# Trainium2, one core: a chunk loop with its state products ahead of the next turn and no special first tiles, SP transfers in another order, attention heads in row tiles of 64

## Chip, cores and metric

The kernel runs on one core of one Trainium2 chip, in one launch. The time is device microseconds (us) for the whole program, the median of a few runs. Engine names are those of the profile: PE is TensorE's matmuls, PEld its weight loads, DVE VectorE, ACT ScalarE, POOL GpSimd, SP SyncE, which here only issues DMA transfers.

## What is computed

Two transformer layers on `x` of 4 sequences of 1024 tokens, width 128, in f32. The first layer's mixer is a gated delta rule with a fast and a slow state per head (16 heads, keys and values of 64), beside a feed-forward layer in emulated FP4. The second layer is causal attention (16 heads of 8) beside a top-1 mixture of 8 experts. Cut to what matters:

```python
def step(carry, x):                       # once a token, S_f = S_s = 0 at a sequence's start
    S_f, S_s = fd * S_f, sd * S_s
    err_f = vt - einsum('bhk,bhkv->bhv', kt, S_f)      # err_s alike
    S_f, S_s = S_f + beta * kt[:, None] * err_f, S_s + beta * kt[:, None] * err_s
    S_fc, S_sc = _cap(S_f + rf * S_s), _cap(S_s + rf * S_f)
    return (S_fc, S_sc), fg * (qt @ S_fc) + sg * (qt @ S_sc)
...
x = x + mixer(layernorm(x)) + fp4_ffn(layernorm(x))
attn = where(triu(k=1), -inf, einsum('bnhd,blhd->bhnl', q, k))
x = x + softmax(SCALE * attn) @ v @ Wp.T + bp + top1_moe(layernorm(x))
```

## The kernel before

The program goes through its stages one after the other. All engines run their own instruction streams, written out in program order and tied by semaphores. By the time in the profiled span: layer norm and FP4 feed-forward (0 to 360 us), projections (360 to 652), key products, gate recurrences on DVE and the transfers that lay their results out (652 to 845), the chunk loop (845 to 2690), output projection, layer norm, routing and experts (2690 to 3061), attention (3061 to 3694) and a last projection.

**The chunk loop.** The 4096 tokens are T = 32 tiles of 128 (TB = 8 to a sequence), and a tile is 4 groups of four heads, so k runs over GROUPS = 128 groups; `first(k)` is true for the groups of tiles 0, 8, 16 and 24, where a sequence starts with a zero state. Inside a tile the delta rule is solved as a triangular system. Its inverse is built up by levels: `lower(k, lv)` (L955) and `update(k, lv)` (L966) on PE for lv 0, 1, 2, with ACT copying each `lower` out (`xs`, L1121) and DVE folding each `update` in (`keep_update`, L1307 for levels 0 and 1, L1305 `tw` for level 2). `solve(k)` (L988) multiplies by that inverse. `turn(k + 1)` (L918) transposes the next group's queries and keys, `states(k, w)` (L978) multiplies the old state `S_t` by keys (w = 0) and queries (w = 1), `scores` (L927) makes the products of keys and queries, `change` (L999) the change of the state, `answers` (L1007) and `values0` (L1016) the output, and `factors` (L936, L939) the decay factors, from `cft`, `lt` and `rt_src`. On DVE `new_state(k - 1, step)` (L1350, L1352, L1354, L1356) forms the new state in steps 0 to 2 and `put_output` (L1374, L1378, L1379) the output; on POOL L853 squares the state and L825 and L826 scale the inverse's parts. `turn(0)` waits for the end of the stage before on each engine (`end_phase`, L479).

The order on PE is `scores(k)`, `change(k-1)`, `lower(k,0)`, `answers(k-1)`, `update(k,0)`, `values0(k-1)`, `lower(k,1)`, `turn(k+1)`, `update(k,1)`, `states(k,0)`, `lower(k,2)`, `states(k,1)`, `update(k,2)`, `factors(k+1)`, `solve(k)`. For a first group `states` and `answers` are left out, `change` is 128 columns narrower, and DVE copies instead of adding.

**SP's queue in the loop.** For tile i SP waits for the tile before last (`av_mm`, `s_new`) and then issues `load_tile(i)` (qkv, `rt_src`, `lt`, `xc`, `blk`, `cft`). Every fourth tile (i = 4, 8, ..., here called a part tile; PT = 4) it also stores the small inverses that DVE worked out during the last four tiles, `store_part(c)` (L650), and loads the next part's blocks, `load_part(c + 1)` (L645), 32 transfers. `INVERSE` spreads the rows of the inverse over the 16 groups of a part.

**Attention.** 32 steps (8 pairs of head sets for 4 sequences), each with 8 query tiles t and 8 key tiles. `for_maxima` (L1849, mask L1851) makes the scores of two heads (e = 0, 1) for a query tile, DVE takes row maxima (L2396), PE turns them (L1859), DVE subtracts them from the queries (`q_less`, L2403), `for_weights` (L1869, mask L1871) makes scores with keys on the rows, ACT takes exponentials (L2087), and `values` (L1887) multiplies by the values. The units share three PSUM slots. Both heads of a pair lie in one 128-row operand, q of head e in rows 64e to 64e + 63; `k_pad` holds k twice, once for each e, with zeros in the other head's 64 rows, so that each matmul contracts over 128 rows:

```python
last = pe.matmul(at[:, e, 0:w], q_parts[:, n, m, t * P:t * P + P], k_pad[:, n, e, m, 512 * c:512 * c + w], ...)
if c == t // 4:
    last = pe.matmul(at[:, e, w - P:w], ident_b[:, :], above[:, :], start=False, stop=True)
```

## Time and profile before

| | |
|---|---|
| median of 3 runs | 3739.81 us |
| lowest and highest | 3722.52 and 3745.09 us |
| the profiled execution's own time | 3714.81 us |
| its span (first to last instruction) | 3713.2 us |
| PE busy | 3009.4 us, 81% of the span |
| DVE, ACT, POOL busy | 70%, 43%, 33% |
| chunk loop, stage 845 to 2690 us | 1845 us |
| attention, stage 3061 to 3694 us | 633 us |

The profile shows one execution. An engine's busy share is an average over stages of different limits; what ends a stretch is read from the row of the instruction that waits. A timeline's row merges consecutive instructions of one line: start, duration, engine, line, operation, operands (for a matmul the tile of weights as rows*columns, here rows of the PE array times columns), count, and in brackets the idle time just before with what ended it. PEclk is the granted clock of TensorE as a share of 2.4 GHz: 1.00 is that level, 0.50 the lower one of 1.2 GHz.

### The profile page before, as it was taken

How to read it: one execution, taken by the hardware profiler on the slowest of the kernel's cores; microseconds unless marked ns; L12 is line 12 of the kernel's file. 1: busy time of each engine (PE TensorE's matmuls, PEld its weight loads, DVE VectorE, ACT ScalarE, POOL GpSimd, SP SyncE). 2: the span in 40 equal slices, each digit the busy share in tenths (PEclk: the TensorE clock that was granted, in tenths of full speed). 3: DMA queues.
4: the chain of work that ended last, by engine and by line, in shares of the span. 5: the costliest groups of instructions: out<-in, count | busy, mean ns of one | idle time of the engine just before them, and what ended most of it. 6: DMA issues, size and time to landing. Idle time of an engine off the chain costs nothing. (4 is left out here: it accounts for less than half of the span.)

```text
span 3713.2 us, 74163 instructions
## 1 busy us (share of the span) xinstructions
PE 3009.4 (81%) x27767; PEld 2108.0 (57%) x27767; DVE 2588.0 (70%) x4506; ACT 1590.6 (43%) x3559; POOL 1226.3 (33%) x1881
## 2 busy tenths in 40 slices
PE   0566999657989979899798997999946388999888
PEld 0444443546767767677676776777735283333334
DVE  8895888873757747587475874766668647777775
ACT  0233999662333323233232332333334254555554
POOL 0000233113545535455354553555546503000000
PEclk9776999885989969899798997999979799999999
DMA  1001665790231312222222222222156322111011
GB/s 28 0 1 61 233 237 243 231 242 30 54 72 35 72 35 60 53 54 62 45 59 54 53 60 47 60 68 46 47 192 211 129 81 45 22 18 27 18 18 32
DMA packets 491495, 290.77 MB, mean 78 GB/s; under 512 B 404955, under 2 KB 451611, under 8 KB 482589
## 3 DMA queue, kind: packets, MB, share of 16 engines
q1 hardware_dynamic: 481920, 256.61, 25.4%
q10 hardware_dynamic: 4608, 16.78, 1.5%
q0 software_dynamic: 4608, 12.59, 1.0%
q8 instruction: 225, 3.69, 0.4%
q14 instruction: 134, 1.10, 0.1%
HBM read 155.92 MB, written 129.97 MB: 77 GB/s over the span
## 5 line engine op out<-in xcount | busy, mean ns | idle before, releaser
L2396 DVE TENSOR_REDUCE mx<-banks 128x2 f32<-128x1024 f32 (+3 forms) x384 | 360.7, 956 | 150.0 <-PE banks L1849 110.7
L2087 ACT ACTIVATE probs<-banks 128x1024 f32<-128x1024 f32 (+3 forms) x384 | 310.2, 811 | 286.6 <-PE banks L1871 156.2
L1121 ACT COPY xs<-banks 64x64 f32<-64x64 f32 (+2 forms) x640 | 166.5, 260 | 597.2 <-PE banks L955 594.2
L1307 DVE SCALAR_TENSOR_TENSOR xc<-xc,halves,banks 64x64 f32<-64x64 f32 (+1 forms) x512 | 160.2, 313 | 271.0 <-PE banks L966 265.2
L955 PE MATMUL banks<-xc,ssm 64*64 64x16 f32 (+2 forms) x5120 | 264.6, 223 | 49.7 <-issue 42.8
L988 PE MATMUL banks<-stk,tw 128*128 128x192 f32 x1024 | 269.5, 422 | 39.2 <-DVE tw L1305 39.2
L955 PEld LDWEIGHTS banks<-xc,ssm 64*64 64x64 f32 x5120 | 222.5, 141 | 127.3 <-issue 63.6
L1729 PE MATMUL banks<-wproj,xnT 128*128 128x512 f32 x512 | 265.4, 600 | 0.9 <-DVE sb_tok L2172 0.9
L1149 ACT COPY ah<-banks 128x768 f32<-128x768 f32 x128 | 102.3, 799 | 381.7 <-PE banks L988 381.7
L826 POOL TENSOR_SCALAR xc<-xc,halves 128x64 f32<-128x64 f32 (+1 forms) x256 | 135.4, 529 | 391.0 <-DVE xc L1307 378.4
L988 PEld LDWEIGHTS banks<-stk,tw 128*128 128x128 f32 x1024 | 220.0, 243 | 64.1 <-DVE tw L1305 59.1
L1111 ACT COPY ssm<-banks 16x64 f32<-16x64 f32 (+2 forms) x896 | 216.7, 242 | 75.6 <-PE banks L927 63.4
L1869 PE MATMUL banks<-q_less,k_pad 128*128 128x512 bf16 (+3 forms) x768 | 204.0, 329 | 51.5 <-DVE mx L2396 50.9
L833 POOL TENSOR_TENSOR ag<-ah,gt_sb 128x512 f32<-128x512 f32 x128 | 174.4, 1363 | 200.1 <-ACT ah L1149 200.1
L1600 POOL TENSOR_TENSOR prj_sq<-prj 128x1024 f32<-128x1024 f32 x32 | 77.5, 2422 | 491.4 <-ACT prj L1990 491.4
L1849 PE MATMUL banks<-k_pad,q_parts 128*128 128x512 bf16 (+3 forms) x768 | 205.5, 331 | 6.3 <-DVE mx L2396 3.3
L966 PE MATMUL banks<-xs,ttw 64*64 64x32 f32 (+1 forms) x3072 | 188.4, 236 | 12.6 <-ACT xs L1121 7.9
L966 PEld LDWEIGHTS banks<-xs,ttw 64*64 64x64 f32 x3072 | 155.1, 148 | 62.4 <-ACT xs L1121 45.4
L1887 PE MATMUL banks<-probs,vaug 128*9 128x256 f32 (+3 forms) x1920 | 184.2, 424 | 0.0
L918 PE MATMUL banks<-ident,qkv_t 128*128 128x128 f32 x512 | 94.0, 312 | 106.8 <-DMA cft<-cf_s 72.5
L927 PE MATMUL banks<-kqt 64*128 64x256 f32 x1024 | 172.6, 463 | 0.0
L1350 DVE TENSOR_TENSOR zs<-S_t,banks 128x256 f32<-128x256 f32 x112 | 47.1, 421 | 179.6 <-PE banks L999 178.7
(351 smaller groups left out, 7012.4 us busy)
## 6 DMA issues: line engine op xcount, KB each, us to landing
proj_s<-prj SPq DMA_DIRECT2D x32, 2048.0 KB, 6.7
qkv_t<-proj_s SPq DMA_DIRECT2D x32, 1536.0 KB
ka<-proj_s ACTq DMA_DIRECT2D x32, 512.0 KB, 4.7
mem_s<-o_sb SPq DMA_DIRECT2D x32, 512.0 KB, 2.6
om<-mem_s SPq DMA_DIRECT2D x32, 512.0 KB, 3.9
om<-proj_s SPq DMA_DIRECT2D x32, 512.0 KB, 4.9
nblk_s<-ssa POOLq DMA_DIRECT2D x32, 256.0 KB, 3.9
blk_s<-res SPq DMA_DIRECT2D x16, 512.0 KB, 4.1
```

The source lines that it names most:

```text
L833: pool.tensor_tensor(ag[:, :, :], ah[:, k % 2, :, 0:P], gt_sb[:, k % 2, :, :], ALU.mult).then_inc(ag_set, 1)
L927: last = pe.matmul(bk[m % 2][:, 256 * p:256 * p + 256], kqt[r, k % 2, p, 0, :], kqt[r, k % 2, p, :, :].rearrange("p w t -> p (w t)"), star ...
L955: last = pe.matmul(products(k, lv, out_)[right, w * m:w * m + w], ssm[rows, lv, m, right], inverse_of(k, lv)[rows, m, :], start=True, stop ...
L966: last = pe.matmul(updates(k, lv, out_)[right, w * m:w * m + w], turned[right, right], xs[right, k % 2, w * m:w * m + w], start=True, stop ...
L988: last = pe.matmul(cols(bk[p], m % 2, P + DK), tw[:, k % 2, m, :], stk[:, k % 2, m, :], start=True, stop=True)
L1111: last = act.copy(ssm[rows, lv, :, right].rearrange("p (k e) t -> p e k t", e=2), both[rows, :, :, right])
L1729: pe.matmul(bank[n], xnT[:, P * i:P * i + P], wproj[:, 512 * n:512 * n + 512], start=True, stop=False)
L1849: last = pe.matmul(at[:, e, 0:w], q_parts[:, n, m, t * P:t * P + P], k_pad[:, n, e, m, 512 * c:512 * c + w], start=True, stop=(c != t // 4))
L1869: last = pe.matmul(at[:, e, 0:end - first], k_pad[:, n, e, m, P * j:P * j + P], q_less[:, s % 2, first:end], start=True, stop=(first != P ...
L1887: last = pe.matmul(bank[6][row:row + SLOT, n0 * P:512], vaug[:, b * TB + j, 2 * (s % 8) + e, :], p_, start=(j == 0), stop=(j == 6 + odd))
L2087: act.activation(probs[:, s % 2, :, at:at + w], slot_of((kind, s, k))[:, :, 0:w], ACT.Exp, scale=D1 ** -0.5).then_inc(b_read, 1)
L2396: dve.tensor_reduce(mx[:, s % 2, c, :, t:t + 1].rearrange("p e a -> p (e a)"), slot_of((kind, s, k))[:, :, 0:w], AX, ALU.max).then_inc(a_r ...
```

## The change

Four edits.

1. **First tiles like all others.** `S_t` is set to zero once by POOL, PE and DVE wait for that (`zero_set` 5), and DVE sets it to zero again in the last tile of a sequence, where the new state would be formed. `states`, `answers`, `keep_states`, the output's terms and the full width of `change` are then run for every group.
2. **Order in a group.** PE's `turn(k + 1)` goes from behind `lower(k, 1)` to behind `lower(k, 2)`, `states(k, 0)` and `states(k, 1)` go ahead and behind `update(k, 1)`. ACT's copies follow. DVE's `new_state(k - 1, 1)` (the second L1352) goes from ahead of `keep_update(k, 2)` to ahead of `keep_update(k, 1)`.
3. **SP.** `load_part(c + 1)` stands behind `load_tile(i)`; `load_part(1)` stands behind the start of the loop instead of in the stage ahead. `r_s` is written in two halves by rows, the first once half of DVE's recurrence is done. The rows of the inverse begin `PART_AT` = 2 groups later in a part.
4. **Attention.** `k_pad` becomes `k_parts`, half as large and without the zeros. Each matmul contracts over 64 rows, head 0 in rows 0 to 63 and head 1 in rows 64 to 127; the two masks follow behind both.

```diff
+        PART_AT = 2
...
-            load_part(1)
...
-            for first_, end in ((0, 2), (2, T)):
-                sp.dma_start(r_s[:, :, :, first_:end, :]...
+            sp.wait_ge(gate_set, 1)
+            sp.dma_start(r_s[:, :, 0:NB, :, :]...).then_inc(gate_out, 16)
...
+            sp.dma_start(r_s[:, :, NB:2 * NB, :, :]...).then_inc(gate_out, 16)
+            sp.wait_ge(gate_out, 64)
...
             end_phase(sp)
+            load_part(1)
...
                 if i % PT == 0:
-                    c = i // PT
                     store_part(c)
-                    if c + 1 < T // PT:
-                        load_part(c + 1)
                     sp.wait_ge(inv_out, 32 * (c + 1))
                 load_tile(i)
+                if i % PT == 0 and c + 1 < T // PT:
+                    load_part(c + 1)
...
+            pool.memset(S_t[:, :, :], 0.0).then_inc(zero_set, 1)
...
+            pe.wait_ge(zero_set, 5)
...
             def states(k, w):
-                if first(k):
-                    return
...
                 if new:
                     lower(k, 1)
+                    states(k, 0)
+                    update(k, 1)
+                    states(k, 1)
+                    lower(k, 2)
                 if more:
                     turn(k + 1)
                 if new:
-                    update(k, 1)
-                    states(k, 0)
-                    lower(k, 2)
-                    states(k, 1)
                     update(k, 2)
...
-                if first(k):
+                if i % TB == TB - 1:
                     if step == 2:
-                        if i:
-                            dve.wait_ge(sq_set, later(k - 4))
-                        dve.tensor_copy(st, ww).then_inc(s_new, 1)
+                        dve.wait_ge(sq_set, later(k))
+                        dve.memset(st, 0.0).then_inc(s_new, 1)
                     return
...
                     put_output(k - 1, 0)
+                    new_state(k - 1, 1)
                 if new:
                     keep_update(k, 1)
                     turn_inverse(k, 1)
                 if old:
                     put_output(k - 1, 1)
-                    new_state(k - 1, 1)
...
                 for e in range(2):
-                    last = pe.matmul(at[:, e, 0:w], q_parts[:, n, m, t * P:t * P + P], k_pad[:, n, e, m, 512 * c:512 * c + w], ...)
-                    if c == t // 4:
+                    rows = slice(64 * e, 64 * e + 64)
+                    last = pe.matmul(at[:, e, 0:w], q_parts[rows, n, m, t * P:t * P + P], k_parts[rows, n, m, 512 * c:512 * c + w], ...)
+                if c == t // 4:
+                    for e in range(2):
                         last = pe.matmul(at[:, e, w - P:w], ident_b[:, :], above[:, :], start=False, stop=True)
```

PE in a regular group, before, from `lower(k, 1)` to `factors(k + 1)` (L955 lower, L918 turn, L966 update, L978 states, L939 factors):

```order
L955 MATMUL banks<-xc,ssm 64x32 x8
L918 MATMUL banks<-ident,qkv_t 128x128 x4
L966 MATMUL banks<-xs,ttw 64x32 x8
L978 MATMUL banks<-S_t,kqt 128x128 x4
L955 MATMUL banks<-xc,ssm 64x64 x4
L978 MATMUL banks<-S_t,kqt 128x128 x4
L966 MATMUL banks<-xs,ttw 64x64 x4
L939 MATMUL banks<-lt,rt_src 128x128 x4
```

The same stretch now (L958 lower, L980 states, L969 update, L921 turn, L942 factors):

```order
L958 MATMUL banks<-xc,ssm 64x32 x8
L980 MATMUL banks<-S_t,kqt 128x128 x4
L969 MATMUL banks<-xs,ttw 64x32 x8
L980 MATMUL banks<-S_t,kqt 128x128 x4
L958 MATMUL banks<-xc,ssm 64x64 x4
L921 MATMUL banks<-ident,qkv_t 128x128 x4
L969 MATMUL banks<-xs,ttw 64x64 x4
L942 MATMUL banks<-lt,rt_src 128x128 x4
```

The turn went down past the level-1 `update`, both `states` and `lower(k, 2)`; the last `update` of a group now stands behind the turn instead of behind a `states`.

DVE in the same group, before (L1374, L1378 and L1379 are the output, L1352 is step 1 of the new state, L1305 the last update's copy `tw`, for which `solve` waits):

```order
L1374 TENSOR_TENSOR oa<-banks,cf 128x2x128 x2
L1307 SCALAR_TENSOR_TENSOR xc<-xc,halves,banks 64x4x32 x2
L1321 STREAM_TRANSPOSE ttw<-xc 32x4x32
L1322 STREAM_TRANSPOSE ttw<-xc 32x4x32
L1378 TENSOR_TENSOR o_sb<-oa 128x2x2x64
L1379 TENSOR_TENSOR o_sb<-o_sb,banks 128x2x2x64
L1352 TENSOR_TENSOR za<-zs,pcb 128x256
L1305 TENSOR_SCALAR tw<-banks 64x4x64
```

And now (L1362, L1366, L1367 the output, L1343 the state, L1297 `tw`):

```order
L1362 TENSOR_TENSOR oa<-banks,cf 128x2x128 x2
L1343 TENSOR_TENSOR za<-zs,pcb 128x256
L1299 SCALAR_TENSOR_TENSOR xc<-xc,halves,banks 64x4x32 x2
L1313 STREAM_TRANSPOSE ttw<-xc 32x4x32
L1314 STREAM_TRANSPOSE ttw<-xc 32x4x32
L1366 TENSOR_TENSOR o_sb<-oa 128x2x2x64
L1367 TENSOR_TENSOR o_sb<-o_sb,banks 128x2x2x64
L1297 TENSOR_SCALAR tw<-banks 64x4x64
```

The state's step 1 went from just ahead of `tw` to ahead of the level-1 update.

SP's queue at tile 4 (a part tile), before (L650 stores a part, L645 loads one, the rest is `load_tile`):

```order
L650 DMA blk_s<-res 128x4x256 x2
L645 DMA res<-nblk_s 16x16x16 x32
L656 DMA qkv_t<-proj_s 128x3072
L674 DMA rt_src<-r_s 16x64x16 x2
L662 DMA lt<-l_s 2x8x16 x16
L666 DMA xc<-blk_s 128x16x16
L668 DMA blk<-blk_s 16x32x16 x8
L680 DMA cft<-cf_s 32x8x16 x2
```

And now (L651 stores, L646 loads a part):

```order
L651 DMA blk_s<-res 128x4x256 x2
L657 DMA qkv_t<-proj_s 128x3072
L675 DMA rt_src<-r_s 16x64x16 x2
L663 DMA lt<-l_s 2x8x16 x16
L667 DMA xc<-blk_s 128x16x16
L669 DMA blk<-blk_s 16x32x16 x8
L681 DMA cft<-cf_s 32x8x16 x2
L646 DMA res<-nblk_s 16x16x16 x32
```

The 32 transfers of L645 went from ahead of the tile's own loads to behind them.

PE at the start of an attention step, before (L1849 and L1869 scores, L1851 and L1871 masks):

```order
L1849 MATMUL banks<-k_pad,q_parts 128x128
L1851 MATMUL banks<-above,ident_b 128x128
L1849 MATMUL banks<-k_pad,q_parts 128x128
L1851 MATMUL banks<-above,ident_b 128x128
L1869 MATMUL banks<-q_less,k_pad 128x384
L1871 MATMUL banks<-below,ident_b 128x128
L1869 MATMUL banks<-q_less,k_pad 128x384
L1871 MATMUL banks<-below,ident_b 128x128
```

And now (L1839 and L1861 scores, L1842 and L1864 masks):

```order
L1839 MATMUL banks<-k_parts,q_parts 128x128 x2
L1842 MATMUL banks<-above,ident_b 128x128 x2
L1861 MATMUL banks<-q_less,k_parts 128x384 x2
L1864 MATMUL banks<-below,ident_b 128x128 x2
```

The two heads' score matmuls now stand next to each other, and the two masks behind them.

## Rows read from the trace of the kernel before

**Rows 1.** windows view by stage: the columns, the chunk loop, the attention

```profile
core 0: us, PE busy (x) PEld busy (x) DVE busy (x) ACT busy (x) POOL busy (x), PEclk, DMA share, GB/s
...
845.00:2690.00 1845.00, 1660.22 (x18567) 1341.74 (x18568) 1214.93 (x2782) 621.02 (x1935) 923.78 (x1651) 0.87 0.24 53
...
3061.00:3694.00 633.00, 568.89 (x4823) 233.28 (x4826) 447.66 (x670) 326.58 (x418) 30.26 (x32) 0.99 0.12 23
```

**Rows 2.** same view: four groups of the first tile of each sequence

```profile
861.72:930.50 68.78, 60.89 (x515) 50.16 (x513) 27.17 (x72) 17.93 (x58) 25.61 (x50) 0.60 0.02 9
...
2265.50:2330.22 64.72, 56.78 (x515) 46.85 (x514) 27.93 (x74) 17.93 (x58) 27.21 (x53) 0.66 0.21 51
sum 266.61, PE 234.96 PEld 193.10 DVE 111.88 ACT 71.73 POOL 107.15; mean PE 58.74 PEld 48.28 DVE 27.97 ACT 17.93 POOL 26.79
```

**Rows 3.** same view: the last 27 groups of the chunk loop

```profile
2330.22:2687.68 357.46, 337.71 (x3993) 272.14 (x3991) 252.68 (x579) 132.41 (x410) 196.74 (x348) 0.95 0.23 56
```

**Rows 4.** same view: two regular groups, one after the other

```profile
1945.19:1957.87 12.68, 12.19 (x149) 9.76 (x149) 9.90 (x23) 5.01 (x16) 7.42 (x14) 1.00 0.01 1
1957.87:1972.19 14.32, 13.56 (x149) 10.92 (x149) 8.91 (x22) 4.97 (x16) 7.25 (x14) 0.88 0.04 17
```

**Rows 5.** same view: the sum over one group at each of six part tiles

```profile
sum 167.05, PE 94.56 PEld 76.17 DVE 58.41 ACT 29.27 POOL 52.55; mean PE 15.76 PEld 12.70 DVE 9.74 ACT 4.88 POOL 8.76
```

**Rows 6.** waits of the chunk loop: us in total, times, longest us

```profile
PE banks L918 <- DMA cft<-cf_s: 72.5, 6, 13.1
...
PE banks L988 <- DVE tw L1305: 39.2, 102, 0.6
```

**Rows 7.** timeline of SP's queue around the load of tile 4

```profile
1038.89 23.88 SPq L645 DMA_DIRECT2D res<-nblk_s  x32
...
1079.70 1.20 SPq L680 DMA_DIRECT2D cft<-cf_s  x2
```

**Rows 8.** DMA view: the store of a part, KB each, median us to landing

```profile
blk_s<-res SPq DMA_DIRECT2D x16, 512.0 KB, 4.1
```

**Rows 9.** timeline of a regular group, four engines

```profile
1949.35 1.16 PE L1007 MATMUL banks<-nycv,ah 128*128 128x128 f32 x8
...
1954.90 0.65 PE L955 MATMUL banks<-xc,ssm 64*64 64x64 f32 x8 [0.27 <-issue]
...
1955.47 0.71 PE L978 MATMUL banks<-S_t,kqt 64*128 64x128 f32 x8
...
1956.36 1.00 DVE L1352 TENSOR_TENSOR za<-zs,pcb 128x256 f32<-128x256 f32 x1
1956.47 0.61 POOL L853 TENSOR_TENSOR sqs<-S_t 128x256 f32<-128x256 f32 x1
...
1957.39 0.43 DVE L1305 TENSOR_SCALAR tw<-banks 64x256 f32<-64x256 f32 x1
...
1957.87 1.43 PE L988 MATMUL banks<-stk,tw 128*128 128x192 f32 x4 [0.18 <-DVE tw L1305]
```

**Rows 10.** windows view: one attention step, cut in two

```profile
3300.34:3307.80 7.46, 6.09 (x56) 3.53 (x56) 6.80 (x14) 4.14 (x7) 0.00 (x0) 1.00 0.11 27
3307.80:3319.49 11.69, 11.65 (x97) 3.68 (x98) 6.87 (x7) 6.03 (x8) 0.00 (x0) 1.00 0.36 51
```

**Rows 11.** timeline of TensorE at the end of an attention step

```profile
3316.09 0.60 PE L1849 MATMUL banks<-k_pad,q_parts 128*128 128x512 bf16 x2
3316.53 0.22 PE L1869 MATMUL banks<-q_less,k_pad 128*128 128x128 bf16 x1
...
3316.70 0.22 PE L1871 MATMUL banks<-below,ident_b 128*128 128x128 bf16 x1
3316.84 0.62 PE L1887 MATMUL banks<-probs,vaug 128*9 128x128 f32 x8
```

**Rows 12.** lines view by form: the largest row maximum of the attention

```profile
L2396 DVE TENSOR_REDUCE mx<-banks 128x2 f32<-128x1024 f32 x192 | 234.9, 1225 | 118.3 <-PE banks L1849 110.7 <-PE banks L1851 6.1
```

**Rows 13.** timeline of SP's queue ahead of the chunk loop

```profile
780.98 22.38 SPq L645 DMA_DIRECT2D res<-nblk_s  x32
```

More of the change, by code:

```diff
@@ L994, in change @@
                 pe.wait_ge(cv_set, k + 1)
-                skip = P if first(k) else 0
-                if not first(k):
-                    pe.wait_ge(ny_set, later(k))
+                pe.wait_ge(ny_set, k + 1)
                 for m, h, r, p in heads(k):
-                    last = pe.matmul(bk[0][r, 256 * p + skip:256 * p + 256], ah[:, k % 2, m, P:P + DK], nycv[:, k % 2, m, skip:256], start=True, stop=True)
+                    last = pe.matmul(bk[0][r, 256 * p:256 * p + 256], ah[:, k % 2, m, P:P + DK], nycv[:, k % 2, m, :], start=True, stop=True)
                 last.then_inc(z_mm, 1)
@@ L1012, in values0 @@
                 pe.wait_ge(ag_set, k + 1)
-                if first(k):
-                    pe.wait_ge(tw_set[0], k + 1)
                 for m, h, r, p in heads(k):
@@ L1163, in chunk_act @@
                     keep_lower(k, 1)
+                    keep_states(k)
+                    keep_lower(k, 2)
                 if more:
                     keep_turned(k + 1)
-                if new:
-                    keep_lower(k, 2)
-                    keep_states(k)
-                if more:
                     keep_factors(k + 1)
@@ L1545, in load_pairs @@
                         rows = slice(64 * e + D1 * m, 64 * e + D1 * m + D1)
-                        for z, level, dst in ((0, of_q[m], q_parts[rows, n, :, :]), (1, of_k[m], k_pad[rows, n, e, :, :])):
+                        for z, level, dst in ((0, of_q[m], q_parts[rows, n, :, :]), (1, of_k[m], k_parts[rows, n, :, :])):
                             src = qk_s[z, level, :, b * L:b * L + L].rearrange("(h d) t -> d h t", d=D1)
@@ L1848, in for_maxima @@
                 for e in range(2):
-                    last = pe.matmul(at[:, e, 0:w], q_parts[:, n, m, t * P:t * P + P], k_pad[:, n, e, m, 512 * c:512 * c + w], start=True, stop=(c != t // 4))
-                    if c == t // 4:
+                    rows = slice(64 * e, 64 * e + 64)
+                    last = pe.matmul(at[:, e, 0:w], q_parts[rows, n, m, t * P:t * P + P], k_parts[rows, n, m, 512 * c:512 * c + w], start=True, stop=(c != t // 4))
+                if c == t // 4:
+                    for e in range(2):
                         last = pe.matmul(at[:, e, w - P:w], ident_b[:, :], above[:, :], start=False, stop=True)
@@ L1868, in for_weights @@
                 for e in range(2):
-                    last = pe.matmul(at[:, e, 0:end - first], k_pad[:, n, e, m, P * j:P * j + P], q_less[:, s % 2, first:end], start=True, stop=(first != P * j))
-                    if first == P * j:
+                    rows = slice(64 * e, 64 * e + 64)
+                    last = pe.matmul(at[:, e, 0:end - first], k_parts[rows, n, m, P * j:P * j + P], q_less[rows, s % 2, first:end], start=True, stop=(first != P * j))
+                if first == P * j:
+                    for e in range(2):
                         last = pe.matmul(at[:, e, 0:P], ident_b[:, :], below[:, :], start=False, stop=True)
@@ L2291, in _ @@
             for n in range(2):
-                for e in range(2):
-                    ones = k_pad[64 * e:64 * e + 64, n, e, :, :].rearrange("p a t -> p (a t)")
-                    dve.tensor_scalar(ones, ones, part[64 * e:64 * e + 64, 4:5], None, ALU.add).then_inc(qk_init, 1)
+                ones = k_parts[:, n, :, :].rearrange("p a t -> p (a t)")
+                dve.tensor_scalar(ones, ones, part[:, 4:5], None, ALU.add).then_inc(qk_init, 1)
             for g in range(T // 4):
```

57 lines of the change are left out of this document (26 added, 31 removed).

## The prediction

> **What bounds the kernel now.** I read the windows view by stage first. Of the 3713.2 us of the span the chunk loop takes 1845 us, with PE busy for 1660 of them, and the attention 633, with PE busy for 569 [rows 1]; the change touches these two and the end of the stage ahead of the loop. In both PE is the engine to look at, so the question for every edit is whether it shortens PE's line or a wait that ends on it.
>
> The loop's rate is read from solve to solve. The last 27 groups take 357.46 us, 13.24 each, at a granted clock of 0.95 [rows 3]. Beneath this mean lie two kinds of group: 12.68 us at clock 1.00 and 14.32 at 0.88, for the same 149 matmul records [rows 4]. Two sorts of group cost much more. The 16 groups of the four first tiles take 266.61 us, 16.7 each, at clock 0.60 to 0.66, with fewer instructions than the rest (515 matmul records in four groups, against 149 in one) [rows 2]. And one group at each of six part tiles takes 27.8 us in the mean, 167.05 for all six [rows 5]. In the waits of the loop these are the six times in which PE's turn waits for `cft`, up to 13.1 us [rows 6]; `cft` is the last transfer of the tile's load.
>
> **First tiles (edit 1).** The row shows fewer matmuls in more time, at a lower clock. PE gets back `states`, `answers` and a wider `change`, and with them the mix of the regular groups, which hold 0.95. So I put them at the regular 13.24: 266.61 - 16 x 13.24 = -54.8 us. Were the clock to stay low for the first group of each tile, some 4 x 4 us would be left. The bound the other way is 12.68 for each group: -63.7. The memset of the state replaces three DVE instructions by one and hides.
>
> **Part tiles (edits 2 and 3).** SP issues the 32 transfers of `load_part` for 23.88 us and only then the tile's own; the last of them, `cft`, is issued at 1079.70 [rows 7]. PE's turn waits 13.1 us at the most [rows 6]. Taking 23.9 us out of the way leaves 10.8 us of slack. The turn comes behind `lower(k, 2)`, some 3 us later in its group: +3. The inverse's rows end two groups later, which by my estimate lets `store_part` begin 1.9 us later: -1.9; and the landing of that store, 4.1 us [rows 8], which `load_part` covered, now stands open. That leaves 10.8 + 3 - 1.9 - 4.1 = 7.8 us, so no stall. `load_part`, now behind the tile's load, ends 42 us after that began (18 from 1062.8 to 1080.9, and 24), and the next tile's transfers are due 53 us (four groups) later: it fits, with 11 us to spare, and DVE uses its blocks only from the third group of the part. What each of the six groups keeps is 13.24: 167.05 - 6 x 13.24 = -87.6 us. The whole loop, from the first solve to the last, is 861.72 to 2687.68: 1825.96 us for 127 groups [rows 2, 3]. At 13.24 each it would be 1681.5, so both terms together with the last 2.1 us elsewhere are -144.5 us.
>
> **The order in a group (edit 2).** Where does a regular group wait? The timeline shows DVE's second L1352 take 1.00 us beside POOL's L853 of 0.61 us, and L1305, which reads the last update, start only behind it at 1957.39; `solve` then starts at 1957.87, having waited 0.18 us for it [rows 9]. In the waits of the loop this is 39.2 us in 102 times, 0.38 each [rows 6]. In the new order L1352 stands ahead of the level-1 copy, where DVE waits for PE's update anyway and POOL doesn't square the state, so `tw` starts with the end of the update, about 0.5 us earlier, and `solve` follows PE's own line. Bounds: 0.2 us (other waits take over) and 0.5 (the weight loads of the solve start earlier too). I take 0.45, near the upper one, since the weight load waits for longer than the matmul does: 127 x 0.45 = -57 us; range -25 to -64. The turn (0.66 us) and `states` (0.71) only change places: between `lower(k, 1)` and `update(k, 1)` stands 0.72 instead of 0.66, between `lower(k, 2)` and `update(k, 2)` 0.66 instead of 0.71, and the 0.27 us ahead of the level-2 `lower` [rows 9] stay. They cost nothing. ACT's copy of the turn goes behind `keep_lower(k, 2)`; the next group's `scores` needs it only after the solve.
>
> **Ahead of the loop (edit 3).** `load_part(1)` goes, 22.38 us of SP's queue [rows 13]. But SP then meets other waits: the zeroing of `blk` by POOL, and the landing of the second half of `r_s`, which now comes ahead of `load_right` and which is some 10 us by transfers of that size. Of the 22 us I keep 3.5, less 1.9 for two memsets that PE now waits for: -1.5 us, between +3.5 and -15.
>
> **Attention (edit 4).** A step is cut in two. In the first 7.46 us PE is busy for 6.09 and DVE for 6.80; in the remaining 11.69 PE is busy for 11.65 and DVE for 6.87 [rows 10]. Only the second is PE's. There two matmuls of 512 columns take 0.44 us from start to start (3316.09 to 3316.53), 0.22 each [rows 11]. If the two heads' matmuls run together, each pair costs one: in that stretch 6016 columns go, 6016 x 0.22 / 512 = 2.6 us. That tiles on different rows do run together the loop shows: eight of L978 on 64 rows take 0.71 us, eight of L1007 on 128 rows with as many columns 1.16 [rows 9]. Against it stands a cost of each change of the tile's shape: from L1871 (128*128) to L1887 (128*9) 0.14 us pass instead of the 0.05 within one form [rows 11], 0.094 as several such pairs agree. The masks stay on 128 rows, so 9 changes come in: +0.85 us. PE's work falls by 1.7 us. A unit there lasts 1.46 us (11.69 / 8) and its row maximum on DVE 1.225 [rows 12], so the last two units can't fall by as much as PE. I take -1.15 us a step, -37 us for 32; bounds 0 (changes cost double) and -2.5, which is -80. The Trainium skill, "TensorEngine Tiling (Array Packing)", Key Properties, says that a change of tiling mode drains TensorE; the trace agrees, with 0.094 us. Its Theoretical Speedup section puts heads of up to 64 rows at up to twice the speed; for the whole step that would be 9216 columns, 3.9 us, 125 us for 32 steps; the trace's 0.71 against 1.16 stays below it. `k_parts` also saves DVE two adds and POOL half a memset: -1.5 us.
>
> **Sum.** -144.5 - 57 - 1.5 - 37 - 1.5 = -241.5 us. The profiled execution took 3714.8 us, so 3473; it is the fastest of those shown, the median is 3739.8, which would give 3498. I put the forecast between: 3485, 12 us over the profile's scale, and add the same 12 to the rivals.
>
> **Rivals.**
> - *Attention gives nothing* (0.17): the changes of shape eat what the pairs save. For it: 9 changes in 11.69 us, and waits that aren't PE's in the other stretch. Against it: the 0.71 of [rows 9]. 3485 + 37 = 3522.
> - *The part tiles still stall* (0.13): the store's landing and the later inverse use up the slack, 6 x 8 us: 3535.
> - *The clock holds 1.00* (0.10): with the turn between two working multiplies no group has its dip; 12.68 instead of 13.24 [rows 3, 4] for 127 groups: -71, 3414.
> - *A dip in every group* (0.07): with the turn next to the level-2 `update`, work of few rows stands together. 14.32 instead of 13.24 for 127 groups: +137, 3622. The Trainium skill, "TensorE: Matmul & The Clock Gate", says in its part on the transpose that PE-mode transposes don't count as activity for the clock; by that the new place of the turn could lengthen the weak stretch. No row here tells the turn's share apart.
> - *Slower* (0.03): the whole loop falls to the mode of the first tiles, 16.7 us a group at clock 0.60 to 0.66 [rows 2]. The place would be the same weak stretch of lower, turn, update and factors, if the clock falls there and doesn't come back before the next one. 127 x 16.7 = 2121 instead of 1826: +295, with -40 from the rest 3714.8 + 255 + 12 = 3982. It decides if the granted clock of the loop is under 0.75: at 15.1 us a group the gain is gone. Against it: the regular groups do as much now and hold 0.95.
>
> The forecast itself has 0.50. About 1% is what a measurement of this kernel can tell from no change, 37 us. Faster by over 1%, thus under 3702, hold the forecast, the first three rivals and the dips: 0.50 + 0.17 + 0.13 + 0.10 + 0.07 = 0.97, less 0.02 for several at once: 0.95. Same 0.02, slower 0.03. The range 3400 to 3575 takes in the first three rivals and the unknown costs of the attention and of `solve`'s wait; it leaves out the last two and a little at either end.
>
> **What would show it.** First tiles at 12.7 to 14.3 us a group and a clock near 0.95; no wait of the turn for `cft`; DVE's L1343 at 0.42 us both times and hardly a wait of `solve` (L990) for L1297; the loop at 1625 us from solve to solve; an attention step of 18.0 us, with pairs of 512-column matmuls in 0.22 us. Wrong would be: a group over 13.5 us in the mean with a clock under 0.93; a step of 19.2; or SP's queue that still ends a wait of PE.

## The result and the profile after

The changed kernel takes 3430.93 us (median of 4 runs, 3427.49 to 3435.30), against 3741.59 us for the kernel before (4 runs, 3722.52 to 3745.09). The ratio is 0.9178, with a 95% interval of 0.9150 to 0.9206: faster by 8.2%. Forecast was 3485, with 3400 to 3575 as the range: inside it, but 54 us faster than the forecast.

The stages again, from the windows view of the changed kernel, to be set beside [rows 1]:

```profile
core 0: us, PE busy (x) PEld busy (x) DVE busy (x) ACT busy (x) POOL busy (x), PEclk, DMA share, GB/s
...
843.00:2413.00 1570.00, 1530.51 (x18943) 1241.29 (x18941) 1189.76 (x2834) 629.35 (x1950) 937.70 (x1647) 0.99 0.28 62
...
2790.00:3410.00 620.00, 527.74 (x4766) 184.11 (x4768) 435.80 (x658) 326.01 (x416) 24.94 (x27) 0.93 0.12 22
```

The loop's stage falls from 1845 to 1570 us and its clock rises from 0.87 to 0.99; PE is busy in 97% of it. The attention falls only from 633 to 620, and its clock is lower than before, 0.93 against 0.99. From marker to marker (first solve, last solve, first and last turn of the maxima), the 282.6 us by which the two profiled spans differ split up as follows:

| part | before | after | difference |
|---|---|---|---|
| start to first solve | 861.7 | 857.2 | -4.5 |
| first to last solve, 127 groups | 1826.0 | 1551.4 | -274.5 |
| last solve to first turn of maxima | 387.5 | 384.7 | -2.8 |
| first to last turn of maxima, 31 steps | 602.3 | 600.9 | -1.4 |
| to the end | 35.7 | 36.4 | +0.7 |

The four first tiles, which answer to [rows 2]:

```profile
857.20:908.28 51.08, 49.85 (x595) 40.31 (x594) 36.18 (x93) 19.69 (x61) 24.22 (x44) 0.96 0.03 4
...
2029.37:2078.29 48.92, 47.69 (x596) 38.67 (x594) 36.45 (x94) 19.69 (x61) 25.30 (x48) 1.00 0.27 58
sum 197.84, PE 192.91 PEld 156.31 DVE 145.53 ACT 78.76 POOL 100.11; mean PE 48.23 PEld 39.08 DVE 36.38 ACT 19.69 POOL 25.03
```

They held 266.61 us at clock 0.60 to 0.66; now 197.84, at 0.96 and 1.00, with 595 matmul records instead of 515. More work takes 69 us less. The last 27 groups [rows 3], and the sum over the groups at the part tiles [rows 5]:

```profile
2078.29:2408.65 330.36, 321.79 (x3992) 261.04 (x3990) 238.55 (x575) 132.15 (x410) 196.46 (x351) 0.99 0.25 62
```

```profile
sum 74.20, PE 72.60 PEld 58.57 DVE 46.67 ACT 29.21 POOL 42.68; mean PE 12.10 PEld 9.76 DVE 7.78 ACT 4.87 POOL 7.11
```

A group in the mean takes 12.24 us instead of 13.24, and the six part groups 12.37 each instead of 27.8; the wait of the turn for `cft` [rows 6] is gone from the waits of the loop, and of those of the solve for `tw` (102 before) one of 0.5 us is left. The timeline of a regular group shows why, PE's and DVE's rows ahead of the solve (L1343 is the state's step 1, L1297 is `tw`, L990 the solve, L855 POOL's square of the state), to be set beside [rows 9]:

```profile
1757.20 0.43 DVE L1343 TENSOR_TENSOR za<-zs,pcb 128x256 f32<-128x256 f32 x1
1757.22 0.66 PE L969 MATMUL banks<-xs,ttw 64*64 64x32 f32 x16
...
1760.36 0.60 POOL L855 TENSOR_TENSOR sqs<-S_t 128x256 f32<-128x256 f32 x1
...
1760.56 0.71 PE L942 MATMUL banks<-lt,rt_src 16*128 16x128 f32 x8
1760.67 0.43 DVE L1297 TENSOR_SCALAR tw<-banks 64x256 f32<-64x256 f32 x1 [0.34 <-PE banks L969]
...
1761.20 0.43 PE L990 MATMUL banks<-stk,tw 128*128 128x192 f32 x1
```

The product stands at 1757.20 and takes 0.43 us instead of 1.00. When POOL squares the state at 1760.36, DVE is past it. `tw` starts at 1760.67 with the end of the update, ends at 1761.10, and the solve starts at 1761.20 with no idle time in brackets.

In the attention, three steps by windows and a piece of one by the timeline (L1839 and L1861 scores, L1842 and L1864 masks, L1880 values), to be set beside [rows 10, 11]:

```profile
3105.60:3123.32 17.72, 16.13 (x154) 5.79 (x153) 13.58 (x21) 10.20 (x13) 0.00 (x0) 1.00 0.27 46
3197.89:3217.85 19.96, 17.60 (x154) 5.84 (x153) 14.28 (x23) 10.20 (x13) 0.00 (x0) 0.91 0.00 1
3237.87:3256.36 18.49, 16.13 (x154) 5.79 (x153) 14.28 (x23) 10.20 (x13) 0.00 (x0) 1.00 0.00 1
```

```profile
3110.34 1.05 PE L1880 MATMUL banks<-probs,vaug 128*9 128x512 f32 x8
3111.32 0.39 PE L1839 MATMUL banks<-k_parts,q_parts 64*128 64x512 bf16 x2
3111.55 0.33 PE L1861 MATMUL banks<-q_less,k_parts 64*128 64x384 bf16 x2
3111.81 0.29 PE L1864 MATMUL banks<-below,ident_b 128*128 128x128 bf16 x2
3112.02 1.04 PE L1880 MATMUL banks<-probs,vaug 128*9 128x384 f32 x8
3113.00 0.28 PE L1839 MATMUL banks<-k_parts,q_parts 64*128 64x256 bf16 x2
```

A step is 17.72 us where it was 19.19. Two matmuls of 512 columns, one on each half of the rows, are one row of 0.39 us, and the next starts 0.23 us after them (3111.32 to 3111.55), where two took 0.44. But of the twelve steps ahead of the last one eight take 19.9 to 20.0 us at clock 0.91, the other four 18.49 at 1.00; in the kernel before all twelve were 19.96 at clock 1.00.

And the first step is not 17.7 us but 46.5. DVE's timeline there:

```profile
2793.07 1.02 DVE L2388 TENSOR_REDUCE mx<-banks 128x2 f32<-128x256 f32 x2
2799.44 1.22 DVE L2395 TENSOR_TENSOR q_less<-q_parts,banks 128x1024 bf16<-128x1024 bf16 x1 [5.35 <-DMA blk_s<-res]
2805.74 0.96 DVE L2388 TENSOR_REDUCE mx<-banks 128x2 f32<-128x768 f32 x1 [5.08 <-DMA res<-nblk_s]
2813.44 1.23 DVE L2388 TENSOR_REDUCE mx<-banks 128x2 f32<-128x1024 f32 x1 [6.74 <-DMA res<-nblk_s]
```

Single instructions, with 5 us between them. This one place costs 29 us and hides the gain of all the others. Whether the change brought it was the first question for the chip.

### The profile page after: what moved, and what is told of

The parts are those of the page before. It is cut to its first block and busy times, and to the rows that moved or that the text cites. A ratio compares the mean times of both kernels' runs of the same rounds, so it can differ in the third digit from the quotient of the medians.

```text
span 3430.6 us, 74926 instructions
## 1 busy us (share of the span) xinstructions
PE 2858.1 (83%) x28151; PEld 1973.1 (58%) x28151; DVE 2554.0 (74%) x4553; ACT 1598.3 (47%) x3575; POOL 1238.9 (36%) x1882
## 5 line engine op out<-in xcount | busy, mean ns | idle before, releaser
L828 POOL TENSOR_SCALAR xc<-xc,halves 128x64 f32<-128x64 f32 (+1 forms) x256 | 193.9, 757 | 359.4 <-DVE xc L1299 346.5
L958 PE MATMUL banks<-xc,ssm 64*64 64x16 f32 (+2 forms) x5120 | 249.9, 217 | 37.1 <-issue 35.0
L958 PEld LDWEIGHTS banks<-xc,ssm 64*64 64x64 f32 x5120 | 209.7, 135 | 116.4 <-issue 57.7
L990 PE MATMUL banks<-stk,tw 128*128 128x192 f32 x1024 | 204.3, 343 | 0.5 <-DVE tw L1297 0.5
L1880 PE MATMUL banks<-probs,vaug 128*9 128x256 f32 (+3 forms) x1920 | 194.2, 446 | 0.0
L1861 PE MATMUL banks<-q_less,k_parts 64*128 64x512 bf16 (+3 forms) x768 | 133.1, 342 | 70.7 <-DVE mx L2388 58.1
L980 PE MATMUL banks<-S_t,kqt 64*128 64x128 f32 x2048 | 184.2, 299 | 0.0
L835 POOL TENSOR_TENSOR ag<-ah,gt_sb 128x512 f32<-128x512 f32 x128 | 162.4, 1269 | 49.4 <-ACT ah L1141 49.2
L990 PEld LDWEIGHTS banks<-stk,tw 128*128 128x128 f32 x1024 | 165.9, 192 | 16.1 <-DVE tw L1297 0.7
L969 PE MATMUL banks<-xs,ttw 64*64 64x32 f32 (+1 forms) x3072 | 171.1, 223 | 0.5 <-ACT xs L1116 0.5
L969 PEld LDWEIGHTS banks<-xs,ttw 64*64 64x64 f32 x3072 | 139.2, 135 | 44.6 <-ACT xs L1116 44.0
L1132 ACT ACTIVATE nycv<-banks 128x512 f32<-128x512 f32 x128 | 76.4, 597 | 180.6 <-PE banks L980 180.6
L1718 PEld LDWEIGHTS banks<-wproj,xnT 128*128 128x128 f32 x512 | 96.6, 191 | 98.8 <-issue 49.8
L1839 PE MATMUL banks<-k_parts,q_parts 64*128 64x512 bf16 (+3 forms) x768 | 134.1, 346 | 21.0 <-ACT probs L2080 11.7
```

The costliest lines, as they stand in the source:

```text
L828: pool.tensor_scalar(inverse_of(k, lv + 1)[:, :, w:2 * w], inverse_of(k, lv), halves[:, lv, 1:2], None, ALU.mult).then_inc(half_set, 1)
L958: last = pe.matmul(products(k, lv, out_)[right, w * m:w * m + w], ssm[rows, lv, m, right], inverse_of(k, lv)[rows, m, :], start=True, stop ...
L969: last = pe.matmul(updates(k, lv, out_)[right, w * m:w * m + w], turned[right, right], xs[right, k % 2, w * m:w * m + w], start=True, stop ...
L980: last = pe.matmul(cols(bk[2 + m % 2], 2 * w + p), kqt[r, k % 2, p, w, :], S_t[r, 2 * g + p, :], start=(w == 0 and p == 0), stop=(w == 0), ...
L990: last = pe.matmul(cols(bk[p], m % 2, P + DK), tw[:, k % 2, m, :], stk[:, k % 2, m, :], start=True, stop=True)
L1718: pe.matmul(bank[n], xnT[:, P * i:P * i + P], wproj[:, 512 * n:512 * n + 512], start=True, stop=False)
```

## The experiments

The twelve kernels ran in three sets of four, each set on one chip beside the kernel before: a to d (kernel before 3708.5 us), e to h (3747.4) and i to l (3744.7). So ratios are compared.

**The four edits one by one.** The first kernel takes the attention edit back, the next three make one edit alone.

```diff
 a_att_undone: the changed kernel, attention as before
-  k_parts[rows, n, m, ...], masks behind both heads
+  k_pad[:, n, e, m, ...], mask behind each head
 b_att_only:   the kernel before
+  k_parts[rows, n, m, ...], masks behind both heads
```

> The changed kernel with the attention edit taken back (padded keys, 128-row matmuls, mask behind each head). Theory 1, from the two profiles: the attention edit gives back in its first step (46.5 us instead of 17.7) what it gains in the others, so it is worth about 1.4 us: the attention takes 602 us from first to last step and its first step 17.7 us, the loop 1551 us, the whole 3432 us. Theory 2: the long first step comes with the whole program and not with the row tiles: the first step is 46 us here too and the whole is 3432 + 29 = 3461 us.

Measured: 3434.6 us beside 3708.5, ratio 0.9261 (0.9236 to 0.9286). First step 17.65 us, attention 602.6, loop 1554.1.

> The kernel before with the attention edit alone. Theory 1: the first step is long wherever the row tiles are: steps of 17.7 us, a first one of 46 us, attention 601 us, the whole within 5 us of the kernel before. Theory 2: the long first step has to do with where the program stands when it gets there (code of another length): first step 17 us, the whole 28 us faster than before.

Measured: 3677.5 us, ratio 0.9915 (0.9886 to 0.9944). First step 17.74 us, attention 571.9: 30 us less than before, and no long step. So the row tiles as such don't make the first step long; what it has to do with was open at this point.

```diff
 c_order_only: the kernel before with the new order in a group (PE, ACT, DVE)
 d_first_only: the kernel before with the first tiles like all others
-                if first(k):
-                    return
```

> The kernel before with the new order of a group on PE, ACT and DVE, first tiles still special. Theory 1: the order alone keeps the granted clock up: regular groups 12.1 us with hardly a dip, so 105 groups x (13.24 - 12.2) = -109 us, and the six part tiles stall 3 us less each, -18 us: 3740 - 127 = 3613 us. Theory 2: the dips are the first tiles' doing: regular groups 12.1 and 13.7 mixed, mean 12.8: -46 - 18, 3676 us.

Measured: 3610.5 us, ratio 0.9736 (0.9709 to 0.9764). The loop takes 1716.2 us. Its last 27 groups:

```profile
2247.83:2578.18 330.35, 321.82 (x3993) 261.26 (x3991) 238.72 (x579) 132.16 (x410) 193.57 (x346) 0.99 0.25 60
```

The same 330.35 us as with the whole change, clock 0.99. The order alone takes the wait of the solve away and most of the dips with it: of the 105 groups that lie neither in a first tile nor at a part tile, 11 take over 13.4 us, 37 in the kernel before, and nine of the eleven stand right beside a first tile or a part tile, whose low clock they share. The first tiles still take 64.6 to 69.3 us, and the part groups 24.4 us in the mean, 3.5 less than before. Theory 1 has the mechanism, that the order alone is enough; in size the 98 us lie between its 127 and the 64 of theory 2.

> The kernel before with the first tiles like all others. Theory 1: the first tiles run at the regular 13.24 us: -55 us, 3685 us, and dips in the other groups as often as before. Theory 2: the full work raises the clock of the first tiles only in part: 15 us a group, -27 us, 3713 us. Theory 3: without special groups the dips vanish everywhere, 12.68 us a group: -55 - 71, 3614 us.

Measured: 3643.5 us, ratio 0.9818 (0.9788 to 0.9848). The first tiles take 49.4 to 51.4 us, the last 27 groups

```profile
2265.73:2615.31 349.58, 330.90 (x3991) 266.99 (x3991) 246.98 (x569) 132.14 (x410) 196.52 (x352) 0.97 0.24 58
```

12.95 each. The loop is 76 us shorter, more than the 55 of theory 1 and less than the 126 of theory 3. The single groups tell where the rest comes from. Where DVE works on a sequence's last tile the changed code forms no new state and so has no product L1352 ahead of `tw`: these groups take 12.17 us at clock 1.00, but for those beside a part tile and, in two of the four sequences, the first of them. The first three groups of the next tile (the very first of the loop apart) take 12.16 to 12.43: there the product is back in its old place, but POOL doesn't square the state in a first tile, and the product takes 0.42 us. From the fourth group on it is 12.67 or 14.3 again. That spoke for the product beside POOL's square as the cause of both the 0.5 us and the dips, and was tested below.

```diff
 e_sp_only: the kernel before with SP's part of the change
                     store_part(c)
-                    if c + 1 < T // PT:
-                        load_part(c + 1)
                     sp.wait_ge(inv_out, 32 * (c + 1))
                 load_tile(i)
+                if i % PT == 0 and c + 1 < T // PT:
+                    load_part(c + 1)
```

> The kernel before with the new order of SP's transfers alone (part loads behind the tile's load, halves of r_s by rows, inverse rows two groups later). Theory 1, the prediction's: 23.9 us leave the way of the tile's load, the slack is 10.8 - 1.9 - 4.1 = 4.8 us with the turn at its old place, so no wait for cft: 6 x (27.8 - 13.2) = -87 us in the loop, the stage ahead of the loop 0 to 5 us shorter: 3620 us where the kernel before has 3708. Theory 2: the later store and its landing use up the slack, some 5 us of each stall stay: -57 us, 3650 us.

Measured: 3646.3 us beside 3747.4, ratio 0.9729 (0.9708 to 0.9751). The groups at the six part tiles take 12.67 to 14.31 us, like any other. The waits of PE in the loop begin

```profile
PE banks L956 <- issue: 42.0, 122, 0.9
PE banks L989 <- DVE tw L1308: 40.3, 108, 0.6
```

with none for `cft`. The slack held even with the turn at its old place. Theory 1 stands; its absolute 3620 us was written for a chip at 3708, and by ratio it becomes 3658. Some of the 12 us below that lie ahead of the loop: the first solve is at 851.8 us, where the kernel before has it at 860.1 to 861.7. And here, in a kernel whose attention nobody touched, the first step took 48.5 us.

**Which part of the order does it.** Two kernels take one engine's order back, a third keeps only DVE's.

```diff
 f_pe_order_old: the changed kernel, on PE
                     lower(k, 1)
-                    states(k, 0)
+                    turn(k + 1)
                     update(k, 1)
-                    states(k, 1)
+                    states(k, 0)
                     lower(k, 2)
-                    turn(k + 1)
+                    states(k, 1)
 g_dve_old: the changed kernel, on DVE
                     put_output(k - 1, 0)
-                    new_state(k - 1, 1)
...
                     put_output(k - 1, 1)
+                    new_state(k - 1, 1)
```

`i_dve_only` is the changed kernel with PE's and ACT's order as before, so that of the new order only DVE's line stays.

> The changed kernel with PE's order in a group as before (turn behind the level-1 lower, both states later), while ACT and DVE keep the new order. Theory 1: it is the place of the turn and the states that holds the clock up: dips come back, 12.1 and 13.7 us mixed, mean 12.7, loop 1551 + 70 = 1620 us, whole 3500. Theory 2: it is the wait of the solve, gone through DVE's order, that held the clock down: loop 1551 us, hardly a dip, whole 3431.

Measured: 3894.7 us, ratio 1.0398 (1.0381 to 1.0415), groups of 16 us. Both theories missed, since the edit itself brought a new wait. ACT kept its new order, with the copy of the states ahead of that of `lower(k, 2)`, while PE made the second states only behind `lower(k, 2)`. Waits of the loop:

```profile
ACT nycv L1132 <- PE banks L980: 372.7, 126, 3.0
PE banks L969 <- ACT xs L1116: 137.2, 126, 1.1
```

ACT waits 3 us a group for the states, and the last update waits 1.1 us for `xs` behind it. So the run can't tell the two theories apart; it says that PE's and ACT's orders of this change belong together. Of the clock it shows one thing: with PE held up by another wait, 1.1 us a group, and hardly a wait of the solve, the clock of the loop is 0.83, lower than the 0.87 of the kernel before [rows 1].

> The changed kernel with DVE's second za product back ahead of tw. Theory 1 (PE's order holds the clock): solve waits 0.4 us a group again, groups 12.5 to 12.6 us without dips, loop 1551 + 50 = 1600 us, whole 3480. Theory 2 (the solve's wait causes the dips): groups 12.68 and 14.3 mixed, mean 13.2, loop 1680 us, whole 3560.

Measured: 3523.6 us, ratio 0.9404 (0.9389 to 0.9420), loop 1648.3 us. The last 27 groups, and the wait of the solve in the loop:

```profile
2154.95:2508.76 353.81, 334.84 (x3990) 270.32 (x3990) 250.94 (x575) 132.40 (x410) 196.57 (x350) 0.96 0.24 57
```

```profile
PE banks L990 <- DVE tw L1297: 43.4, 101, 0.5
```

The wait is back, 0.43 us each time, and with it 12.68 us a group and a dip in more than one of five (28 groups of 14.2 to 14.7 us in the loop; the changed kernel has two over 13.5, the first of the loop among them). Theory 1 had the clock held up by PE's order, which falls; theory 2 holds, a little weaker than written: 13.1 us in the mean.

This run also has a control within itself. In a sequence's first tile POOL doesn't square the state, while DVE's product stands ahead of `tw` as everywhere. A group there, and one just behind that tile:

```profile
1291.13:1303.25 12.12, 11.85 (x150) 9.62 (x149) 7.99 (x21) 4.88 (x15) 6.66 (x13) 1.00 0.36 37
1315.84:1328.52 12.68, 11.92 (x151) 9.63 (x149) 10.01 (x27) 5.09 (x16) 7.20 (x14) 1.00 0.05 20
```

and the rows ahead of the solve that ends each:

```profile
1302.29 0.42 DVE L1343 TENSOR_TENSOR za<-zs,pcb 128x256 f32<-128x256 f32 x1
1302.77 0.43 DVE L1297 TENSOR_SCALAR tw<-banks 64x256 f32<-64x256 f32 x1
1303.25 1.57 PE L990 MATMUL banks<-stk,tw 128*128 128x192 f32 x8
...
1327.00 1.00 DVE L1343 TENSOR_TENSOR za<-zs,pcb 128x256 f32<-128x256 f32 x1
1327.11 0.60 POOL L855 TENSOR_TENSOR sqs<-S_t 128x256 f32<-128x256 f32 x1
1328.03 0.43 DVE L1297 TENSOR_SCALAR tw<-banks 64x256 f32<-64x256 f32 x1
1328.52 1.57 PE L990 MATMUL banks<-stk,tw 128*128 128x192 f32 x8 [0.50 <-DVE tw L1297]
```

Same order, same work on PE: without the square the product takes 0.42 us, the solve doesn't wait, and the group takes 12.12; with it 1.00, a wait of 0.50, and 12.68. So it isn't the place of the product alone that costs, but the place beside POOL's square.

> The changed kernel with PE's and ACT's order in a group as before; of the new order only DVE's earlier za product is kept. Theory 1 (the solve's wait is what made both the 12.68 us and the dips): groups 12.1 us with hardly a dip, loop about 1555 us, the whole as the changed kernel. Theory 2 (PE's order has a share): the wait is gone but dips return, 12.1 and 13.7 us mixed, mean 12.7, loop 1620 us. Theory 3: the product at its new place is late for the old order (stalls at the level-1 copy): groups over 12.5 us without a wait of the solve.

Measured: 3442.9 us beside 3744.7, ratio 0.9193 (0.9173 to 0.9214); the changed kernel, unchanged, in the same set 0.9192. Loop 1564.5 us, 11 more than with PE's order. The last 27 groups:

```profile
2091.44:2423.32 331.88, 322.55 (x3992) 261.35 (x3990) 238.70 (x575) 132.51 (x410) 199.49 (x355) 0.99 0.25 61
```

Theory 1 stands: with one DVE instruction moved ahead of the six that stood before it, PE's and ACT's new order adds hardly anything. A full-clock group is 12.17 us instead of 12.11, four of the 105 regular groups take over 13.4 instead of one, and the medians, 3442.9 and 3441.2, don't tell the two kernels apart. A kernel with the other three edits and the whole old order wasn't run.

**The first attention step.**

```diff
 h_gather_late: the changed kernel, on POOL
+            pool.wait_ge(m_mm, 5)
             for t in range(T):
                 pool.indirect_dma_start(xnT1[...], None, ys_s[:, :], ...)
```

> The changed kernel; POOL's second series of 32 indirect transfers (xnT from ys_s) waits until the fifth attention step instead of starting with the first. Theory 1: the 29 us in the first attention step are a collision with these transfers, which needs the two to start together: first step 17.7 us, no long step later, whole 3431 - 29 = 3402 us. Theory 2: any attention step beside these transfers can be caught: a long step of 40 us or more appears where the transfers now run. Theory 3: the transfers have nothing to do with it: first step 46.5 us as now, 3431 us.

Measured: 3442.5 us, ratio 0.9197 (0.9180 to 0.9214). Steps 16.8, 18.8, 17.7, 17.7, then 56.2 for the fifth, the one beside which the 32 transfers now run (2862.56 to 2902.29 on POOL's timeline), then 17.7. DVE's timeline has the longest wait there:

```profile
2907.81 2.09 DVE L2389 TENSOR_REDUCE mx<-banks 128x2 f32<-128x1024 f32 x2 [23.11 <-DMA res<-nblk_s]
```

Theory 2: the cost goes where the transfers go, 38.5 us there.

```diff
 k_before_same, l_after_same: both kernels, unchanged, profiled in one set
```

> The kernel before, unchanged, profiled on the same chip as the next three. Theory 1 (the 29 us in the first attention step belong to the chip or the execution, whatever the kernel): first step long here if and only if it is long in the unchanged new kernel of this set, and the time is then near 3745 us with it and near 3710 us without. Theory 2 (they belong to the program): first step 17.7 us here as in its first profile, and 46.5 us in the new kernel of the same set.

> The changed kernel, unchanged, in the same set. Theory 1: its first step is long if and only if that of the kernel before is; without it the time is 3431 - 29 = 3402 us and the ratio to before 0.917. Theory 2: first step 46.5 us, 3431 us.

Measured: 3745.8 us for the kernel before (ratio to its other runs 1.0003, 0.9988 to 1.0019) and 3441.2 for the changed one (0.9192, 0.9170 to 0.9214). DVE's timeline in the kernel before, in this set:

```profile
3071.61 1.22 DVE L2403 TENSOR_TENSOR q_less<-q_parts,banks 128x1024 bf16<-128x1024 bf16 x1 [6.39 <-DMA blk_s<-res]
3078.59 0.96 DVE L2396 TENSOR_REDUCE mx<-banks 128x2 f32<-128x768 f32 x1 [5.76 <-DMA res<-nblk_s]
3088.38 1.23 DVE L2396 TENSOR_REDUCE mx<-banks 128x2 f32<-128x1024 f32 x1 [8.84 <-DMA res<-nblk_s]
3099.61 0.43 DVE L2396 TENSOR_REDUCE mx<-banks 128x2 f32<-128x256 f32 x1 [10.00 <-DMA res<-nblk_s]
```

The window around it:

```profile
3064.30:3095.00 30.70, 5.73 (x26) 2.62 (x26) 4.28 (x5) 0.00 (x0) 22.65 (x24) 0.56 0.23 56
```

The same picture in the old kernel: its first step is 47.83 us, its attention 632.6, and its span 3732.6 where the profile shown ahead of the prediction had 3713.2 and no long step. Theory 1 stands: the 29 us belong to the chip or the execution and not to the change. The profiles of the four kernels of the first set have no such step, those of the eight in the two other sets all have it, whatever was changed in them. With both profiles from one set, the table above reads -1.5, -263.5, -7.3, -31.5 and +0.6 us, in sum -303.1, and the attention's gain is there to see. Why these chips differ stays open.

**A further step.** Both masks made of matmuls on 64 rows too, so that scores and masks have one shape.

```diff
 j_masks_64: the changed kernel
-                    for e in range(2):
-                        last = pe.matmul(at[:, e, w - P:w], ident_b[:, :], above[:, :], start=False, stop=True)
+                    for z in range(2):
+                        for e in range(2):
+                            rows = slice(64 * e, 64 * e + 64)
+                            last = pe.matmul(at[:, e, w - P:w], ident_2[rows, z, :], above_2[rows, z, :], start=False, stop=(z == 1))
```

> The changed kernel with the masks too as matmuls on 64 rows: each mask in two halves, the heads beside each other, so that a score and its mask have one shape. It takes 12 small transfers ahead of the attention. Theory 1 (the changes of shape are what the pairs give back): 16 changes a step x 0.094 us go, of which about half lie on the path that PE sets: steps of 17.0 us instead of 17.7, the attention 25 us shorter. Theory 2 (DVE's maxima and the exponentials set the pace now): steps stay at 17.7 us, same time. Theory 3: more busy rows also lift the clock in the last steps, from 20.0 to 18.5 us: another 12 us.

Measured: 3421.4 us, ratio 0.9133 (0.9111 to 0.9154), beside 0.9192 for the changed kernel: another 20 us. One step:

```profile
3100.00:3117.06 17.06, 14.58 (x188) 5.78 (x186) 13.59 (x21) 10.21 (x13) 0.00 (x0) 1.00 0.01 2
```

17.06 us, PE busy for 14.58 where it was 16.13. Theory 1 is right: 0.66 us a step, and 20 us from the first to the last turn of the maxima. Of theory 3 little is left: dips of 19.4 against 17.83 us stay, five in the twelve steps instead of eight. Something of the gain goes elsewhere: between the two profiles the stretch from the last solve to the attention is 394 us instead of 380, which would fit the 12 transfers ahead, and the loop 6 us longer, so these two executions differ by only 4 us, while the medians differ by 20.

## Why the prediction came out as it did

**First tiles.** Right in kind: with the full work the clock is that of all others. Forecast -54.8 us at 13.24 a group; measured 266.6 to 197.8, -68.8, since a group is now 12.2 and not 13.24. In the old order of a group (d) it is -65.3. The one group that stayed slow is the very first of the loop, 14.27 us.

**Part tiles.** Right: no wait for `cft`, 167.05 to 74.20 us, -92.9 where -87.6 was forecast plus the 0.45 us of each. The slack of 7.8 us itself wasn't measured; that the transfers alone with the old turn don't stall shows that the 4.8 us left without the turn's 3 were enough.

**The order in a group.** Here is the step that failed. Mechanism and place were right: the doubled L1352 beside POOL's L853, the late `tw`, the waiting solve. The Trainium skill, "SBUF — State Buffer", section "SBUF: two separate sides", has a rule for it: VectorE with two inputs in SBUF and a GpSimd instruction that reads SBUF lock each other out on a shared port, and the one that starts first keeps it. The trace agrees with the first half: 0.42 us alone and 1.00 beside L853, in all 108 such pairs of the kernel before. The second half doesn't show in the recorded starts: DVE's product begins 0.11 us ahead of L853 in all 108 pairs, and yet it is DVE's that is stretched, to 0.28 us past the end of L853, which keeps its 0.61.

The size was off twice, and together that is the term that failed. Of the loop's -274.5 us, -68.8 are the first tiles' and -92.9 the part tiles'; the other -112.8 are 105 groups that fell by 1.07 us each, where the forecast took 0.45. The full-clock group went from 12.68 to 12.11, -0.57 for the -0.45 taken. And the dips went with the wait: the forecast counted on 13.24 - 0.45, while the rival "the clock holds 1.00", at 0.10, had the 0.56 us of dips, but put it down to the place of the turn. In i the turn stands at its old place and hardly a group dips. g and i show that both come from one cause: where DVE's product stands ahead of `tw`, the solve waits and many groups take 14.1 to 14.7 us (35 before, 28 in g); where it doesn't (i, the changed kernel), the solve doesn't wait and no more than 4 behind the first take over 13.4. c, whose first and part tiles are still slow, has 11, nine of them beside these. 12.68 - 0.45 = 12.23 for 127 groups is 1553 us, and the measured loop has 1551.45; that this comes so close is luck in part, a full-clock group at 12.11 with some of 12.4 to 12.6 and two dips among them. The two terms should have been one case. How a wait of 0.4 us in a group leads to the lower clock no run here shows; that both go and come together is what they show.

**Dip in every group and the slow mode.** Neither came. With the turn between `lower(k, 2)` and `update(k, 2)` the loop ran at a clock of 1.00 over all its 1551 us. By what the Trainium skill, "TensorE: Matmul & The Clock Gate", says on the PE-mode transpose, and the prediction set beside the dips, this place looked weak; no row shows a loss there. In the slow mode's bound a sum was off: the gain would be gone at (1826 + 40) / 127 = 14.7 us a group, not 15.1.

**Attention.** Forecast -37 us from -1.15 a step; measured -30.4 (b) and -31.5 (k and l). A step without a dip gains 1.47 us, more than taken. A change of shape costs what it was put at: the mask's start behind two scores of 384 columns is 0.26 us (3111.55 to 3111.81) for 0.16 of columns. PE's busy time in a step fell by 1.61 us, from 17.74 [rows 10] to 16.13, where the forecast had 1.7 in the second stretch alone and took a part of it off again for the last two units' maxima; how the 1.47 is shared between the two stretches wasn't read out. What was not foreseen are the twelve steps ahead of the last: in eight of them the clock is 0.91, which in the kernel before no step behind the first has, and these take 19.9 to 20.0 us, as much as before. That takes back 1.5 us in eight steps, 12 us. It comes with the attention edit (b has it, a has not); what in it lowers the clock wasn't tried.

**Ahead of the loop.** -1.5 forecast, -4.5 in the first pair and -1.5 in the last; e alone has the first solve at 851.8 against 860 to 862. Inside the bounds.

**The scale.** The forecast of 3485 lay 12 us over the profile's scale. That profile had no long first step, and its 3714.8 us lie under three of the four other runs, 3739.8 to 3745.1, by about what the step costs; the fourth took 3722.5. That those three had it is inferred, since they have no profile. It would explain why the change is -283 us between the first two profiles and -311 between the medians. From the median of 3741.6 the forecast's own sum of -241.5 gives 3500, 69 us over what was measured. That 3485 came within 54 is owed to the scale chosen, and in part luck.

## What to carry to other kernels

When an instruction of another engine stands just ahead of the one that the busiest engine waits for, look at its longest instances and not at its median: here 1.00 us against 0.42, in one of its two places only, and only beside one POOL instruction. When a change takes a short wait of PE away and the granted clock dips in the same loop, price the two together: here both went with the same DVE instruction. And profile both kernels in one set before reading a stage's difference: 29 us of one stage came and went with the chip.

## What was not expected of the hardware

- While POOL issues its 32 indirect transfers (1.25 us each, 40 us together), in two of three sets the engines that wait for PE start 5 to 23 us after its recorded end. At 2794.36 PE's last turn of the maxima ends, at 2799.44 DVE's `q_less`, which waits for it, starts; ACT's table load for its first exponential starts only at 2824.7, the scores being done at 2801.8, and POOL's issue of its last transfer ends at 2822.9. PE's start behind DVE stays at 0.1 us. The ends of matmuls are modelled in the profile, so whether PE's result or only the news of it is late isn't shown. It follows the transfers to another step (56.2 us, h) and doesn't depend on the kernel (k). In the first set the same transfers beside the same steps cost nothing.
- First tiles with 515 matmul records in four groups ran at 0.60 to 0.66 and took 64.7 to 68.8 us; with 593 and the order of a group unchanged (d) they take 49.4 to 51.4 at 0.96 to 1.00; in the changed kernel, with 595, it is 48.9 to 51.1. The form that leaves work out was the slower one.
- Two matmuls on rows 0 to 63 and 64 to 127 start 3 to 5 ns apart and take the time of one; against 128-row matmuls 0.23 us for the pair of 512 columns instead of 0.44.
